# Audio tower on one core: centring and variance of chunks two and three of the output projection placed in the feed-forward loop

## Chip, cores and metric

The kernel runs on one core of one Trainium2 chip. The metric is the time of one execution on the device in microseconds (us), from the first to the last instruction; lower is better. Engines are named as in the profile: PE is TensorE, DVE VectorE, ACT ScalarE, POOL GpSimd, SP SyncE, which issues most DMAs. "Slow" and "full" clock of PE are its two granted levels, 1.2 and 2.4 GHz (0.50 and 1.00 in the profile).

## What is computed

Three blocks run over 2048 tokens (32 sequences of 64) with 1024 features: a token block (projection, layernorm, five-tap convolution, feed-forward), attention, and a grouped feed-forward. The change lies between the last two:

```python
h = tok(x)                                             # 2048 x 1024
h = h + attn(layernorm(h), w_qkv, b_qkv, w_o, b_o)     # ends in vals @ w_o.T + b_o
h = h + ffn(layernorm(h), up, down, perm)

def _layernorm(x, axis=-1, eps=1e-05):
    m = jnp.mean(x, axis=axis, keepdims=True)
    v = jnp.var(x, axis=axis, keepdims=True)
    return (x - m) / jnp.sqrt(v + eps)

def ffn(x, up, down, perm):                            # 16 heads, 64 -> 256 -> 64
    t = x[:, perm].reshape(-1, 16, 64)
    t = einsum('bhd,hdm->bhm', t, up)
    t = gelu(t)
    t = einsum('bhm,hmd->bhd', t, down)
    return t.reshape(-1, 1024)[:, argsort(perm)]
...
```

## The kernel before, in words

Features lie on the 128 partitions in 8 blocks (k or m = 0 to 7), tokens along the free axis in 4 chunks (c = 0 to 3) of 512. All matrix work is fp32; the projections split each operand into a high and a low part and take three matmuls per product (`split3`). Each engine runs its own written-out program, and semaphores alone tie them together, so the order of lines in an engine's block is the order on its queue.

**Projection stage** (780 to 889 us of the profile). For each chunk PE runs three groups of output blocks (0-2, 3-5, 6-7). DVE's `o_evac` (L1350) adds bias and residual into `h2[c % 2]`; SP stores that to HBM (`h2_s[c]`). The sum over features is made by POOL (`o_sum` L737, blocks 1 to 4) and then DVE (`o_sum` L1358, blocks 5 to 7); PE turns it into a mean (`stat_mean_pe` L383) in the next chunk, and ACT copies it out (`stat_copy_act` L370). The deviations of chunk c - 1 are then worked out during chunk c, block by block: DVE centres (`stat_center` L377), ACT squares (L381), POOL adds the squares up (`ln_var_add` L335). The buffer `sq` between them has two slots, so DVE waits for POOL from the third block on. PE reduces the result (`stat_var_pe` L397, eight matmuls of one column into bank 3 here), ACT takes the root (L406), DVE the reciprocal (L410), and SP stores it and reads it back broadcast (`d_stat_load`, tiles `mtd`, `rtd`).

**Feed-forward loop** (889 us to the end): 32 steps s = 8c + a. In step s PE runs `ff_up` of block s + 1 (L1795) into banks 0-3, and `ff_down` of block s (L1804) into bank 4 or 5; ACT runs four gelus (L1077); DVE adds the result of step s - 1 to the gathered block (`d_add` L1408) and prepares a block of the next chunk (`d_prep` L1377, L1384); POOL issues the scatter of the finished block (L758) and the gather (L752), an indirect DMA of 256 KB, of a block of the chunk after. `hg` holds two chunks. Chunk 3's centring runs in this loop, a block per step from s = 5 (`STAT_FROM`), its mean on PE at s = 1 and its variance matmuls at s = 12. Chunk 2's centring runs in the projection of chunk 3, its variance matmuls behind that projection's last group, and the second half of `ff_up` of block 0, which needs bank 3, waits for its root.

Of the kernel before, what the change touches and what calls it, by code (L numbers as in the profile page):

```python
# [32 lines left out]
def audio_tower(nc, x_t, w_proj, w_ff, w_gen, w_qkv_t, w_o_t, up, down, vecs, perm, *outs):  # L33
# [12 lines left out]
    with ctx:  # L46
# [5 lines left out]
        def sem(name):  # L52
# [98 lines left out]
        hg = place("hg", [P, 2 * KB, N], F32, R2 + 16 * KIB)  # L151
# [20 lines left out]
        ln_pool, ln_mean, ln_d, ln_sq, ln_var, ln_std, ln_rstd = (  # L172
            sem(s) for s in ("ln_pool", "ln_mean", "ln_d", "ln_sq", "ln_var", "ln_std", "ln_rstd"))
# [130 lines left out]
        def ln_sum_pool(g, L, blk):  # L304
            g.tensor_tensor(acc[:, :], blk(0), blk(1), ALU.add).then_inc(ln_pool, 1)
            for k in range(2, KB):
                since(g, ln_pool, L, 14, k - 1)
                g.tensor_tensor(acc[:, :], acc[:, :], blk(k), ALU.add).then_inc(ln_pool, 1)  # L308

        def ln_mean_pe(pe, L):  # L310
            since(pe, ln_pool, L, 14, 7)
# [8 lines left out]
        def ln_square_act(act, L, k, d):  # L320
            since(act, ln_d, L, 8, k + 1)
            if k >= 2:
                since(act, ln_pool, L, 14, 7 + max(1, k - 2))
# [5 lines left out]
        def ln_var_add(g, L, k):  # L329

            since(g, ln_sq, L, 8, k + 1)
            if k > 1:
                since(g, ln_pool, L, 14, 7 + k - 1)
            t = squares(L)
            g.tensor_tensor(vacc[:, :], t[:, 0, :] if k == 1 else vacc[:, :], t[:, k % 2, :],  # L335
                            ALU.add).then_inc(ln_pool, 1)
# [5 lines left out]
        def ln_var_pe(pe, L):  # L342
            since(pe, ln_pool, L, 14, 14)
# [28 lines left out]
        def stat_center(e, L, S, k, src):  # L372
            if k == 0:
                since(e, st_copied, S, 1, 1)
            if k >= 2:
                since(e, ln_pool, L, 14, 7 + max(1, k - 2))
            e.tensor_tensor(sq[:, k % 2, :], src, mean_t[:, :], ALU.subtract).then_inc(ln_d, 1)  # L377

        def stat_square_act(act, L, k):
            since(act, ln_d, L, 8, k + 1)  # L380
            act.activation(sq[:, k % 2, :], sq[:, k % 2, :], ACT.Square).then_inc(ln_sq, 1)  # L381

        def stat_mean_pe(pe, L):  # L383
            since(pe, ln_pool, L, 14, 7)
# [4 lines left out]
        def stat_var_pe(pe, L, S, b=LN_BANK):  # L389
            since(pe, ln_pool, L, 14, 14)  # L390
# [25 lines left out]
        def _(sp):  # L416
# [213 lines left out]
            for c in range(CH):  # L630
# [10 lines left out]
                if c > 0:  # L641
# [4 lines left out]
            d_stat_load(1)  # L646
            d_stat_load(2)
# [9 lines left out]
        def _(g):  # L657
# [85 lines left out]
            def gather(n, ks=range(KB)):  # L743
# [1150 lines left out]
```

## Time and profile before

| | |
|---|---|
| median of 3 runs | 1031.88 us (1027.65 to 1033.29) |
| profiled execution | 1035.96 us, of which the span from first to last instruction 1034.2 us |
| PE busy | 967.4 us, 94% of the span |
| DVE, ACT, POOL busy | 509.2, 424.4, 394.3 us |
| DMA | 124.96 MB, 121 GB/s on average |

Times in the rows below are microseconds from the span's start in the profiled execution. A row of a timeline has start, duration, engine, line of the code, operation, output<-inputs, count, and in brackets the idle time of the engine just before and what ended it. Rows of consecutive equal instructions are merged. A fp32 matmul shows as two entries, so `ff_up` of one block (4 matmuls) is x8, and so is `ff_down`.

### The profile page before, as it was taken

What the parts mean: (1) busy time and instruction counts of PE and PEld (TensorE: products, weight loads), DVE (VectorE), ACT (ScalarE), POOL (GpSimd) and SP (SyncE); (2) the same over time, 40 slices, a digit from 0 to 9 for tenths busy, and PEclk for the clock granted to TensorE, in tenths of its full rate; (3) what the DMA queues carried; (4) which work ended last, traced back from release to release, by engine and by line L of the source; (5) the groups of instructions that cost most, each with busy time, mean ns of one, the idle gap of its engine ahead of it and who ended that gap; (6) DMA issues with size and microseconds to landing.
All of it is one profiled execution on the core that took longest, in us unless ns stands there. A gap on an engine that the chain in (4) does not pass through costs nothing.

```text
span 1034.2 us, 15644 instructions
## 1 busy us (share of the span) xinstructions
PE 967.4 (94%) x6108; PEld 714.5 (69%) x6108; DVE 509.2 (49%) x848; ACT 424.4 (41%) x753; POOL 394.3 (38%) x317
## 2 busy tenths in 40 slices
PE   7999999987899999999879999999999999889996
PEld 5777777776777788778657877877887777323331
DVE  6153535659447502254756256256064567755551
ACT  6144444555433533434243243243132332356553
POOL 1225252227601122723361451451023377748532
PEclk9999999999899999999989999999999999899998
DMA  8542725395343154327100201200214975533421
GB/s 290 209 165 4 205 7 181 4 285 203 117 145 107 62 126 164 109 95 265 41 11 22 92 11 35 79 11 22 92 52 149 289 260 209 184 111 133 149 77 61
DMA packets 75062, 124.96 MB, mean 121 GB/s; under 512 B 29159, under 2 KB 38375, under 8 KB 70894
## 3 DMA queue, kind: packets, MB, share of 16 engines
q1 hardware_dynamic: 68830, 107.03, 33.7%
q0 software_dynamic: 5120, 16.78, 4.6%
q8 instruction: 48, 0.79, 0.3%
q10 hardware_dynamic: 1040, 0.16, 0.1%
q14 instruction: 24, 0.20, 0.1%
HBM read 81.46 MB, written 42.50 MB: 120 GB/s over the span
## 4 chain that ended last, share of the span: by engine, by line
PE 53%; issue 10%; POOL 7%; DVE 5%; DMA 3%; ACT 2%; another core or an unknown queue 1%; POOLq 0%; SPq 0%; DVEq 0%; ACTq 0%
PE bank L299 14%; PE bank L301 13%; PE bank L300 13%; PE bank L1795 3%; PE bank L1804 3%; POOL vacc L335 2%; PE bank L1551 1%; POOL out L758 1%; POOL acc L363 1%; DVE sq L377 1%; DMA stage<-w_qkv_t 1%; POOL acc L308 1%; DVE acc L1219 1%; PE bank L1523 1%; DMA db_late<-h_s 1%
## 5 line engine op out<-in xcount | busy, mean ns | idle before, releaser
L335 POOL TENSOR_TENSOR vacc<-vacc,sq 128x512 f32<-128x512 f32 x72 | 97.2, 1350 | 45.8 <-ACT sq L381 36.4
L299 PE MATMUL bank<-xa_h,wp_h 128*128 128x512 f32 x256 | 103.4, 404 | 7.2 <-DVE xa_l L1094 7.2
L299 PE MATMUL bank<-cv_h,wf_h 128*128 128x512 f32 x256 | 106.3, 415 | 1.2 <-POOL wf_l L293 1.2
L301 PE MATMUL bank<-cv_h,wf_l 128*128 128x512 f32 x256 | 101.4, 396 | 0.0
L300 PE MATMUL bank<-cv_l,wf_h 128*128 128x512 f32 x256 | 101.4, 396 | 0.0
L300 PE MATMUL bank<-xa_l,wp_h 128*128 128x512 f32 x256 | 101.1, 395 | 0.0
L301 PE MATMUL bank<-xa_h,wp_l 128*128 128x512 f32 x256 | 101.1, 395 | 0.0
L700 POOL TENSOR_TENSOR fo<-fo,res 128x512 f32<-128x512 f32 x32 | 43.5, 1373 | 123.4 <-ACT fo L837 89.8
L1077 ACT ACTIVATE gt<-bank 128x512 f32<-128x512 f32 x128 | 66.2, 600 | 39.0 <-PE bank L1795 36.8
L1795 PE MATMUL bank<-dd,up_f 64*128 64x512 f32 x256 | 67.9, 651 | 5.6 <-ACT gt L1077 5.4
L381 ACT ACTIVATE sq<-sq 128x512 f32<-128x512 f32 x56 | 35.1, 632 | 79.3 <-DVE sq L377 79.3
L1804 PE MATMUL bank<-gt,dn_f 128*64 128x512 f32 x256 | 62.5, 611 | 0.0
L299 PEld LDWEIGHTS bank<-xa_h,wp_h 128*128 128x128 f32 x256 | 48.9, 191 | 18.9 <-DVE xa_l L1094 7.2
L299 PEld LDWEIGHTS bank<-cv_h,wf_h 128*128 128x128 f32 x256 | 48.9, 191 | 14.1 <-issue 2.8
L299 PE MATMUL bank<-xc_h,wq_h 128*128 128x512 f32 x128 | 54.3, 425 | 3.9 <-issue 3.9
L300 PEld LDWEIGHTS bank<-xa_l,wp_h 128*128 128x128 f32 x256 | 49.0, 191 | 10.8 <-issue 0.7
L301 PEld LDWEIGHTS bank<-cv_h,wf_l 128*128 128x128 f32 x256 | 48.9, 191 | 10.7
L301 PEld LDWEIGHTS bank<-xa_h,wp_l 128*128 128x128 f32 x256 | 48.9, 191 | 10.6
L300 PEld LDWEIGHTS bank<-cv_l,wf_h 128*128 128x128 f32 x256 | 49.0, 191 | 10.5 <-issue 1.2
L758 POOL DMA_INDIRECT out<-hg,rows x32 | 35.3, 1103 | 53.5 <-DVE hg L1408 51.4
L1795 PEld LDWEIGHTS bank<-dd,up_f 64*128 64x128 f32 x256 | 22.4, 194 | 47.9 <-issue 42.2
L1408 DVE TENSOR_TENSOR hg<-bank,hg 128x512 f32<-128x512 f32 x32 | 22.1, 690 | 66.2 <-PE bank L1804 60.1
(179 smaller groups left out, 2167.5 us busy)
## 6 DMA issues: line engine op xcount, KB each, us to landing
xs<-x_t SPq DMA_DIRECT2D x32, 256.0 KB, 6.2
h_s<-ho SPq DMA_DIRECT2D x8, 1024.0 KB, 5.9
res<-h_s SPq DMA_DIRECT2D x32, 256.0 KB, 3.6
h_s<-fo SPq DMA_DIRECT2D x32, 256.0 KB, 2.4
dc<-h_s SPq DMA_DIRECT2D x4, 2048.0 KB, 9.3
h<-h_s SPq DMA_DIRECT2D x8, 1024.0 KB, 10.5
h_s<-h SPq DMA_DIRECT2D x8, 1024.0 KB, 4.8
stage<-w_qkv_t SPq DMA_DIRECT2D x24, 256.0 KB, 3.6
```

The lines of the kernel that those rows point to most:

```text
L299: pe.matmul(o, wh, xh, start=start, stop=False)
L300: pe.matmul(o, wh, xl, start=False, stop=False)
L301: return pe.matmul(o, wl, xh, start=False, stop=stop)
L308: g.tensor_tensor(acc[:, :], acc[:, :], blk(k), ALU.add).then_inc(ln_pool, 1)
L335: g.tensor_tensor(vacc[:, :], t[:, 0, :] if k == 1 else vacc[:, :], t[:, k % 2, :], ALU.add).then_inc(ln_pool, 1)
L381: act.activation(sq[:, k % 2, :], sq[:, k % 2, :], ACT.Square).then_inc(ln_sq, 1)
L700: g.tensor_tensor(fo[m % 4][:, :], fo[m % 4][:, :], res[:, m % 2, :], ALU.add).then_inc(ff_add, 1)
L758: g.indirect_dma_start(out=outs[c], out_offset=bass.IndirectOffsetOnAxis(ap=rows[:, k:k + 1], axis=0), in_=hg[:, hg_block(c) + k, :], in_o ...
L1077: act.activation(gt[a % 2][:, i, :], bank[i][:, :], ACT.Gelu).then_inc(gelu_ok, 1)
L1408: v.tensor_tensor(dst, bank[4 + a % 2][:, :], dst, ALU.add).then_inc(d_ev, 1)
L1795: mm = pe.matmul(bank[2 * blk + j][:, :], up_f[r, a, cols], dd[r, a, :], start=True, stop=True)
L1804: pe.matmul(bank[4 + a % 2][side, :], dn_f[:, FFB * a + 2 * head + blk, :], gt[a % 2][:, i, :], start=blk == 0, stop=blk == 1).then_inc(g_ ...
```

## The change

Chunks are counted from 0, so the third and fourth are c = 2 and 3. Centring of both runs in the loop, two blocks a step, at s = 0 to 3 (c = 2) and s = 8 to 11 (c = 3), into a tile of eight slots, `sq8`. ACT squares them one step later, POOL adds them two steps later. The variance matmuls stand behind steps 6 and 14, in bank 7, the first followed by chunk 3's mean. The semaphore `ln_pool` is split in two (`ln_sum`, `ln_vac`), since sums and variances no longer alternate. `hg` becomes three buffers; the gather of chunk 1 moves from behind the projection into it, ahead of POOL's sum of chunk 3. The preparation of chunk 0 is wholly in the projection of chunk 3, ahead of the evacuations of groups 0 and 1. DVE's `o_sum` moves ahead of the last `o_low`. The store and read-back of chunk 2's deviations move behind `d_stat_load(1)`. Preparation and gather in the loop start a step later (4 and 5 for 3 and 4).

```diff
-        hg = place("hg", [P, 2 * KB, N], F32, R2 + 16 * KIB)
+        hg = [place(f"hg{i}", [P, KB, N], F32, at)
+              for i, at in enumerate((R2 + 32 * KIB, R1 + 48 * KIB, R2 + 16 * KIB))]
+        sq8 = place("sq8", [P, KB, N], F32, E + 16 * KIB)
...
         def ln_var_add(g, L, k):
             since(g, ln_sq, L, 8, k + 1)
             if k > 1:
-                since(g, ln_pool, L, 14, 7 + k - 1)
+                since(g, ln_vac, L, 7, k - 1)
...
         def stat_center(e, L, S, k, src):
             if k == 0:
                 since(e, st_copied, S, 1, 1)
-            if k >= 2:
-                since(e, ln_pool, L, 14, 7 + max(1, k - 2))
-            e.tensor_tensor(sq[:, k % 2, :], src, mean_t[:, :], ALU.subtract).then_inc(ln_d, 1)
+            if L == 3 * CH - 1:
+                since(e, ln_vac, L - 1, 7, max(1, k))
+            elif L < 3 * CH - 2 and k >= 2:
+                since(e, ln_vac, L, 7, max(1, k - 2))
+            dst = sq8[:, k, :] if L >= 3 * CH - 2 else sq[:, k % 2, :]
+            e.tensor_tensor(dst, src, mean_t[:, :], ALU.subtract).then_inc(ln_d, 1)
...
# SP
-                if c > 0:
+                if 0 < c < CH - 1:
                     stat_store(CH + c - 2, 1)
...
             d_stat_load(1)
+            stat_store(2 * CH - 3, 1)
             d_stat_load(2)
...
# POOL
                 if n == 1:
+                    g.wait_ge(qk_mm, 8 * CH)
+                if n == 2:
                     g.wait_ge(o_mm, 8 * CH)
                 for k in ks:
-                    if n >= 2:
-                        g.wait_ge(d_st[k], 16 * (n - 1))
+                    if n == 3:
+                        g.wait_ge(d_st[k], 32)
...
                 if c == 3:
                     gather(0, range(4, KB))
-                ln_var_pool(g, 2 * CH + c - 1)
+                    gather(1)
+                if c < CH - 1:
+                    ln_var_pool(g, 2 * CH + c - 1)
                 o_sum(c)
-            gather(1)
             for s in range(CH * KB + 1):
-                k = s - STAT_FROM
-                if 0 < k < KB:
-                    ln_var_add(g, 3 * CH - 1, k)
+                for i, steps in enumerate(CENTERS):
+                    for k in steps.get(s - 2, ()):
+                        if k > 0:
+                            ln_var_add(g, 3 * CH - 2 + i, k)
...
# ACT
-                    for k in range(KB):
+                    for k in range(KB if c < CH - 1 else 0):
                         stat_square_act(act, L, k)
...
                 gelus(s // KB, s % KB)
-                if s == 2:
+                for i, steps in enumerate(CENTERS):
+                    for k in steps.get(s - 1, ()):
+                        stat_square_act(act, L - 1 + i, k)
+                if s == VAR_AT[0] + 1:
+                    stat_std_act(act, L - 1, FF_VAR_BANK)
                     stat_copy_act(act, L, 2 * CH - 2)
-                if 0 <= s - STAT_FROM < KB:
-                    stat_square_act(act, L, s - STAT_FROM)
-                if s == STAT_FROM + KB:
-                    stat_std_act(act, L)
+                if s == VAR_AT[1] + 1:
+                    stat_std_act(act, L, FF_VAR_BANK)
...
# DVE
-                if c > 0:
+                if 0 < c < CH - 1:
                     o_center(c - 1, range(4))
+                if c == CH - 1:
+                    d_prep(0, range(4))
                 o_evac(c, A_GROUPS[0])
-                for k in range(4, KB) if c > 0 else ():
-                    o_center(c - 1, [k])
-                    if c == CH - 1:
-                        d_prep(0, [k - 4])
+                if 0 < c < CH - 1:
+                    o_center(c - 1, range(4, KB))
+                if c == CH - 1:
+                    d_prep(0, range(4, KB))
                 o_evac(c, A_GROUPS[1])
                 if c + 1 < CH:
                     o_low(c + 1, range(PAIRS - 1))
                 o_evac(c, A_GROUPS[2])
+                o_sum(c)
                 if c + 1 < CH:
                     o_low(c + 1, [PAIRS - 1])
-                o_sum(c)
...
-                d_prep(0, LAST_PREP.get(s, ()))
-                if s == 0:
-                    stat_recip_dve(v, 3 * CH - 2)
-                if 0 <= s - STAT_FROM < KB:
-                    o_center(CH - 1, [s - STAT_FROM])
-                if s == STAT_FROM + KB:
-                    stat_recip_dve(v, 3 * CH - 1)
+                for i, steps in enumerate(CENTERS):
+                    o_center(CH - 2 + i, steps.get(s, ()))
+                    if s == VAR_AT[i] + 2:
+                        stat_recip_dve(v, 3 * CH - 2 + i)
...
# PE
-                        if c > 0 and (g, k) == (2, 3):
+                        if 0 < c < CH - 1 and (g, k) == (2, 3):
                             pe.wait_ge(o_ev, 8 * c + VAR_BANK + 1)
                             stat_var_pe(pe, 2 * CH + c - 1, CH + c - 2, VAR_BANK)
...
             for blk in range(2):
-                if blk == VAR_BANK // 2:
-                    pe.wait_ge(ln_std, 3 * CH - 1)
                 ff_up(0, 0, blk)
...
-                if s == 1:
+                for i in range(2):
+                    if s == VAR_AT[i]:
+                        stat_var_pe(pe, 3 * CH - 2 + i, 2 * CH - 3 + i, FF_VAR_BANK)
+                if s == VAR_AT[0]:
                     stat_mean_pe(pe, 3 * CH - 1)
-                if s == STAT_FROM + KB - 1:
-                    stat_var_pe(pe, 3 * CH - 1, 2 * CH - 2)
...
-LAST_PREP = {0: (4, 5), 1: (6, 7)}
-PREP_AFTER, STAT_FROM, GATHER_AFTER = 3, 5, 4
+CENTERS = ({0: (0, 1), 1: (2, 3), 2: (4, 5), 3: (6, 7)},
+           {8: (0, 1), 9: (2, 3), 10: (4, 5), 11: (6, 7)})
+VAR_AT, FF_VAR_BANK = (6, 14), 7
+PREP_AFTER, GATHER_AFTER = 4, 5
```

## Rows read from the trace of the kernel before

**Rows 1.** The page, section 1: busy time, share of the span, instructions

```profile
PE 967.4 (94%) x6108; PEld 714.5 (69%) x6108; DVE 509.2 (49%) x848; ACT 424.4 (41%) x753; POOL 394.3 (38%) x317
```

**Rows 2.** Timeline of PE where the projection ends and the loop begins

```profile
881.77 0.39 PE L301 MATMUL bank<-vs_h,wo_l 128*128 128x512 f32 x1
886.91 2.00 PE L397 MATMUL bank<-mean_w,vacc 128*128 128x1 f32 x8 [4.75 <-DVE h L1354]
...
894.58 1.94 PE L1804 MATMUL bank<-gt,dn_f 128*64 128x512 f32 x8
```

**Rows 3.** Timelines of POOL and DVE over the same boundary

```profile
882.10 1.71 POOL L335 TENSOR_TENSOR vacc<-vacc,sq 128x512 f32<-128x512 f32 x1 [1.29 <-ACT sq L381]
...
885.60 3.38 DVE L1354 SCALAR_TENSOR_TENSOR h<-bank,vec,h 128x512 f32<-128x512 f32 x5
```

**Rows 4.** Windows of 2 us: busy by engine, PE clock, DMA share, GB/s

```profile
874.00:876.00 2.00, 2.00 (x11) 1.65 (x10) 1.97 (x3) 0.63 (x1) 0.76 (x1) 1.00 0.00 0
...
888.00:890.00 2.00, 2.00 (x8) 1.47 (x10) 0.98 (x2) 1.04 (x2) 1.71 (x3) 0.50 1.03 375
...
902.00:904.00 2.00, 2.00 (x10) 0.55 (x10) 0.69 (x1) 0.00 (x0) 1.40 (x2) 1.00 0.92 327
...
910.00:912.00 2.00, 2.00 (x8) 0.52 (x6) 0.00 (x0) 1.31 (x3) 0.00 (x0) 0.50 0.21 74
```

**Rows 5.** Timeline of PE and ACT in the loop's first steps

```profile
900.23 1.12 PE L385 MATMUL bank<-acc,mean_w 128*128 128x512 f32 x2
...
904.01 0.60 ACT L370 ACTIVATE mean_t<-bank 128x512 f32<-128x512 f32 x1 [4.32 <-remote]
...
908.01 2.93 PE L1795 MATMUL bank<-dd,up_f 64*128 64x512 f32 x8 [2.87 <-ACT gt L1077]
910.87 2.67 PE L1804 MATMUL bank<-gt,dn_f 128*64 128x512 f32 x8
```

**Rows 6.** Timeline of PE late in the loop: two steps, and its end

```profile
1011.54 1.99 PE L1795 MATMUL bank<-dd,up_f 64*128 64x512 f32 x8
...
1015.33 1.99 PE L1795 MATMUL bank<-dd,up_f 64*128 64x512 f32 x8
...
1021.03 3.65 PE L1804 MATMUL bank<-gt,dn_f 128*64 128x512 f32 x16
```

**Rows 7.** Timeline of PE around the variance matmuls of step 12, and the window behind

```profile
946.85 2.01 PE L1795 MATMUL bank<-dd,up_f 64*128 64x512 f32 x8 [0.58 <-ACT gt L1077]
...
951.16 2.03 PE L397 MATMUL bank<-mean_w,vacc 128*128 128x1 f32 x8 [0.44 <-POOL vacc L335]
953.12 3.60 PE L1795 MATMUL bank<-dd,up_f 64*128 64x512 f32 x8
...
954.00:956.00 2.00, 2.00 (x8) 0.63 (x4) 0.00 (x0) 1.74 (x3) 1.70 (x2) 0.50 0.69 212
```

**Rows 8.** Windows of 4 us behind the variance matmuls of chunks 0 and 1

```profile
830.00:834.00 4.00, 4.00 (x18) 3.48 (x19) 4.00 (x4) 0.78 (x2) 3.71 (x3) 1.00 0.21 75
...
858.00:862.00 4.00, 4.00 (x12) 3.11 (x11) 3.56 (x4) 0.59 (x2) 3.71 (x3) 0.60 0.04 13
```

**Rows 9.** Timeline of POOL: a gather in the projection, the eight of chunk 1 (first, last)

```profile
867.47 1.26 POOL L752 DMA_INDIRECT hg<-h_s,rows  x1 [0.30 <-issue]
...
892.41 0.96 POOL L752 DMA_INDIRECT hg<-h_s,rows  x1
...
901.44 0.95 POOL L752 DMA_INDIRECT hg<-h_s,rows  x1 [0.30 <-issue]
```

**Rows 10.** DMA issues: output<-input, queue, count, us from issue to landing

```profile
hg<-h_s,rows POOLq DMA_INDIRECT x32, 5.4
```

**Rows 11.** Timelines of ACT and POOL in the loop: table load, four gelus, one addition

```profile
951.58 1.28 ACT L406 ACT_TABLE_LOAD   x1
...
959.73 2.06 ACT L1077 ACTIVATE gt<-bank 128x512 f32<-128x512 f32 x4 [1.89 <-PE bank L1795]
...
949.82 1.28 POOL L335 TENSOR_TENSOR vacc<-vacc,sq 128x512 f32<-128x512 f32 x1
```

More of the change, by code:

```diff
@@ L171, in audio_tower @@
         a_st = [sem(f"a_st{g}") for g in range(2)]
-        ln_pool, ln_mean, ln_d, ln_sq, ln_var, ln_std, ln_rstd = (
-            sem(s) for s in ("ln_pool", "ln_mean", "ln_d", "ln_sq", "ln_var", "ln_std", "ln_rstd"))
+        ln_sum, ln_vac, ln_mean, ln_d, ln_sq, ln_var, ln_std, ln_rstd = (
+            sem(s) for s in ("ln_sum", "ln_vac", "ln_mean", "ln_d", "ln_sq", "ln_var", "ln_std", "ln_rstd"))
         st_copied, mean_st, rstd_st = sem("st_copied"), sem("mean_st"), sem("rstd_st")
@@ L304, in ln_sum_pool @@
         def ln_sum_pool(g, L, blk):
-            g.tensor_tensor(acc[:, :], blk(0), blk(1), ALU.add).then_inc(ln_pool, 1)
+            g.tensor_tensor(acc[:, :], blk(0), blk(1), ALU.add).then_inc(ln_sum, 1)
             for k in range(2, KB):
-                since(g, ln_pool, L, 14, k - 1)
-                g.tensor_tensor(acc[:, :], acc[:, :], blk(k), ALU.add).then_inc(ln_pool, 1)
+                since(g, ln_sum, L, 7, k - 1)
+                g.tensor_tensor(acc[:, :], acc[:, :], blk(k), ALU.add).then_inc(ln_sum, 1)
         def ln_mean_pe(pe, L):
-            since(pe, ln_pool, L, 14, 7)
+            since(pe, ln_sum, L, 7, 7)
             since(pe, ln_std, L - 1, 1, 1)
@@ L322, in ln_square_act @@
             if k >= 2:
-                since(act, ln_pool, L, 14, 7 + max(1, k - 2))
+                since(act, ln_vac, L, 7, max(1, k - 2))
             act.activation(squares(L)[:, k % 2, :], d, ACT.Square).then_inc(ln_sq, 1)
@@ L332, in ln_var_add @@
             if k > 1:
-                since(g, ln_pool, L, 14, 7 + k - 1)
-            t = squares(L)
-            g.tensor_tensor(vacc[:, :], t[:, 0, :] if k == 1 else vacc[:, :], t[:, k % 2, :],
-                            ALU.add).then_inc(ln_pool, 1)
+                since(g, ln_vac, L, 7, k - 1)
+            t, at = (sq8, k) if L >= 3 * CH - 2 else (squares(L), k % 2)
+            g.tensor_tensor(vacc[:, :], t[:, 0, :] if k == 1 else vacc[:, :], t[:, at, :],
+                            ALU.add).then_inc(ln_vac, 1)
         def ln_var_pool(g, L):
@@ L342, in ln_var_pe @@
         def ln_var_pe(pe, L):
-            since(pe, ln_pool, L, 14, 14)
+            since(pe, ln_vac, L, 7, 7)
             since(pe, ln_d, L, 8, 8)
@@ L361, in stat_sum_pool @@
             if k > 1:
-                since(g, ln_pool, L, 14, k - 1)
-            g.tensor_tensor(acc[:, :], blk(0) if k == 1 else acc[:, :], blk(k), ALU.add).then_inc(ln_pool, 1)
+                since(g, ln_sum, L, 7, k - 1)
+            g.tensor_tensor(acc[:, :], blk(0) if k == 1 else acc[:, :], blk(k), ALU.add).then_inc(ln_sum, 1)
         def stat_copy_act(act, L, S):
@@ L374, in stat_center @@
                 since(e, st_copied, S, 1, 1)
-            if k >= 2:
-                since(e, ln_pool, L, 14, 7 + max(1, k - 2))
-            e.tensor_tensor(sq[:, k % 2, :], src, mean_t[:, :], ALU.subtract).then_inc(ln_d, 1)
+            if L == 3 * CH - 1:
[4 more added lines that the diff above has]
+            e.tensor_tensor(dst, src, mean_t[:, :], ALU.subtract).then_inc(ln_d, 1)
         def stat_square_act(act, L, k):
             since(act, ln_d, L, 8, k + 1)
-            act.activation(sq[:, k % 2, :], sq[:, k % 2, :], ACT.Square).then_inc(ln_sq, 1)
+            d = sq8[:, k, :] if L >= 3 * CH - 2 else sq[:, k % 2, :]
+            act.activation(d, d, ACT.Square).then_inc(ln_sq, 1)
         def stat_mean_pe(pe, L):
-            since(pe, ln_pool, L, 14, 7)
+            since(pe, ln_sum, L, 7, 7)
             pe.matmul(bank[LN_BANK][:, :], mean_w[:, :], acc[:, :], start=True, stop=True).then_inc(ln_mean, 1)
         def stat_var_pe(pe, L, S, b=LN_BANK):
-            since(pe, ln_pool, L, 14, 14)
+            since(pe, ln_vac, L, 7, 7)
             since(pe, st_copied, S, 1, 1)
@@ L922, in b_step @@
                     act.wait_ge(mean_st, 16 * (CH - 1))
-                    act.wait_ge(ln_pool, 14 * (CH - 1))
+                    act.wait_ge(ln_vac, 7 * (CH - 1))
                 if c == 1:
@@ L1361, in o_sum @@
                     v.wait_ge(o_ev, 8 * c + m + 1)
[L1362 to L1363 removed]
+                    v.wait_ge(ln_sum, 7 * (2 * CH + c) + m - 1)
+                    v.tensor_tensor(acc[:, :], acc[:, :], h2[c % 2][:, m, :], ALU.add).then_inc(ln_sum, 1)
             def o_center(c, ks):
```

18 lines of the change are left out of this document (7 added, 11 removed).

## Prediction

> **What bounds the kernel now.** I read the page's busy times first: PE is busy 94% of the span [rows 1], so time can come back only where PE stands still, works at the slow clock, or does side work. Then PE's timeline from the last projection on, for every gap above 0.3 us, and the windows of 2 us for its clock and the DMAs. A step of the loop takes 3.79 us at full clock (1011.54 to 1015.33), and the last `ff_down` ends at 1021.03 + 3.65 = 1024.68 [rows 6]. From the first `ff_down`, at 894.58 [rows 2], 32 steps of which the last has no `ff_up` would take 31 x 3.79 = 117.3 us; they take 130.1. Four places hold what is lost:
>
> - **The boundary.** The projection's last matmul ends at 882.16. PE then stands 4.75 us, runs chunk 2's variance matmuls for 2.0 us, and reaches the first `ff_down` at 894.58, 12.4 us later [rows 2]. What ends the wait is DVE's evacuation, five blocks at once at 885.60 that could have been done as banks filled [rows 3]; it had stood behind the centring, and that behind POOL's additions, 1.71 us each and 1.29 us of wait between [rows 3]. The clock is at 0.50 when the loop starts [rows 4].
> - **First steps.** The mean costs 1.06 us. Then ACT gets it only at 904.01, 2.7 us after PE's record ends, released by something the trace doesn't name; PE stands 2.87 us, and the next step takes 2.93 + 2.67 for 3.79 [rows 5], at clock 0.50 [rows 4]. I call this the **unnamed stall**: 2.87 + 1.7 = 4.6 us.
> - **Centring of chunk 3.** With two slots, DVE, ACT and POOL go in lockstep, and every second step PE waits 0.58 us for a gelu [rows 7]; four or five such waits make 2.5 us.
> - **Variance at step 12**: 0.44 us of wait, 2.0 us of matmuls, and an `ff_up` of 3.60 us for 1.99 behind them, at clock 0.50: 4.1 us [rows 7].
>
> 1.1 + 4.6 + 2.5 + 4.1 = 12.3 of the 12.8 us lost in the loop.
>
> **The change, part by part.**
>
> *Boundary.* DVE has no centring left there, only preparations and evacuations at 0.68 us each [rows 3]. `ff_up` of block 0 needs bank 3 evacuated by 882.16 and a prepared block, and `ff_down` banks 4 to 7 by 884.1. With preparation ahead of evacuation, DVE needs eight operations for blocks 4 to 7 (5.4 us) and one evacuation (0.7) after those gathers have landed: free if they land by 876.0. The fourth is issued at 867.47 [rows 9] and lands 5.4 us later by the median of all gathers [rows 10]; in the kernel before the DMA engines had nothing left in flight at 874 [rows 4]. Cost 0, at most 1 us, since chunk 1's gathers queue behind. Then `ff_up` of block 0 starts at 882.16 and takes 1.9 us; by the pattern of the loop its gelus start 1.2 us in and the first two end at 884.4, `ff_up` of block 1 runs to 886.4, and the first `ff_down` starts there, not at 894.58. PE never idles over 0.5 us, so I take the clock as full. **Gain 8.2 us** (7 to 8.5).
>
> *What POOL does instead.* It loses seven additions and issues twelve gathers in a row ahead of its sum of chunk 3. The first four end at 868.7; eight more at 1.29 us (892.41 to 901.44, seven intervals) or at the 1.56 us of the row in the projection end at 879.0 to 881.2 [rows 9]. Four additions of 1.28 [rows 11] to 1.71 us [rows 3] end at 884.1 to 888.0; DVE's three behind them, 2.0 us, at 886.2 to 890.1. **Queued behind that wait on DVE** are the first centrings, behind these on ACT two squares, and behind those the gelus of block 2, which `ff_up` of block 3 wants at about 892.1. Counting back two gelus, two squares and two centrings (1.0, 1.2, 1.3) the sum must be over by 888.4. Cost 0 to 1.7 us, and I take 0, because the gathers in one unbroken row are the nearer case to the eight at 1.29.
> The 2 MB of these gathers fall into a time when the DMA engines are idle (0.00 at 874 to 876) and leave one when they carry 327 GB/s (902 to 904) [rows 4].
>
> *The unnamed stall.* It stands in the middle of the eight gathers' traffic and the read-backs of the statistics. Both are gone from there. I take it as gone, with 3 in 10 that it is of another making and comes again.
>
> *Mean* moved: 1.06 us either way. *Variance*: one group leaves the boundary (counted), one is new behind step 6, one moves from 12 to 14. Each is 2.0 us of matmuls, and a clock that falls: 1.6 us at `ff_up` [rows 7], and the same for a group in the projection, 0.60 in the window behind chunk 1's, but not behind chunk 0's, 1.00 [rows 8]. Two groups: 4.0 + 3.2 = 7.2 us for 3.6 before. The wait for POOL: after step 6 it has finished long before. For step 14, POOL has in steps 10 to 13 seven additions and four pairs of scatter and gather. At 1.28 and 2 x 1.3 us that is 19 us, at 1.71 and 2 x 1.56 us 24 us; the last pair stands behind the last addition, so 16.8 to 21.3 us count against 4 steps and a step's own length, 18.9 us: 0 to 2.4 us of wait. I take 0.
> POOL's addition takes 1.71 us beside DVE in the projection [rows 3] and 1.28 us in the loop [rows 11]. The Trainium skill, page "GPSIMD Engine Reference", section "Key points", says that POOL shares its SBUF interfaces with VectorE and contends with DVE instructions that have two SBUF inputs. That speaks against this change, which puts two such centrings a step beside the additions; by it the upper figures would hold, and the sum be about 2 us longer.
>
> *Lockstep.* With eight slots DVE waits for no addition. DVE's step holds at most five operations, 3.4 us, and ACT's four gelus and two squares, 2.06 [rows 11] + 1.2 = 3.3 us, both under 3.79, and each engine's urgent work comes first in its step. Gain 2.5 us and the 0.44. The two more table loads, 1.28 us each [rows 11], fall where ACT has over 1.7 us spare and PE is at its variance matmuls: 0, at most 0.5 us.
>
> *Rest.* `o_sum` ahead of the last `o_low`: the mean matmul that PE runs next hides it, 0 (0.3 us at most). SP: `d_stat_load(2)` now waits for a reciprocal at step 8, is needed at step 12, 15 us for a store and a load. `d_stat_load(1)` no longer waits. Gathers for the third buffer come seven steps before use. All 0.
>
> **The sum.** First `ff_down` 886.4; + 117.3 + 1.1 (mean) + 7.2 (variance) + 0.5 (unassigned before) = 1012.5 for the end of PE, against 1024.68: **12.2 us**. The tail behind it (9.5 us, scatters landing) stays. The profiled execution would go from 1035.96 to 1023.8. That execution lies 4.1 us above the median, about one unnamed stall, so the median runs may never have had it: then their gain is 7.6 us. 1031.88 - 12.2 = 1019.7, 1031.88 - 7.6 = 1024.3. I forecast **1021.5 us**, nearer to the first.
>
> **The rivals.**
>
> 1. *The stall comes again* (or is absent from the median of before, same result): 1024.3. For it: the trace doesn't name its releaser. Against: its place in the DMA traffic.
> 2. *The clock holds behind the variance groups.* 3.2 us less, 1016.5 to 1018. For it, chunk 0's group [rows 8]; against it, the other two. By the Trainium skill, page "TensorE: Matmul & The Clock Gate", section "Why this matters for your kernels", throughput drops come from long idle gaps between bursts of matmuls; by that the clock would hold here, where PE idles 0.44 us at most.
> 3. *POOL becomes the bound.* Upper prices in both places: 1.7 + 2.4 us, and a fallen clock behind each wait, 3.3 us: 1027 to 1029, within 0.5% of before. For it: POOL's rows of 1.71; against: POOL's additions in the loop all near 1.28.
> 4. *Slower: the evacuation stands behind late gathers.* DVE's preparation of blocks 4 to 7 is in front of the evacuation of banks 3 to 7, and PE waits us for us once they land after 876.0. The gain is used up at 888, and over 0.5% lost if they land after 893, 25 us after issue: 1038 or more. Against: 5.4 us by the median [rows 10].
> 5. *The change doesn't do what it says*: PE still stands at the boundary for some other evacuation, at half of the gain: 1026. DVE's free time of 2.7 us there speaks against it.
>
> **How the numbers follow.** Forecast case 0.5, rival 1 0.2, rival 2 0.12, rival 3 with rival 5 0.13, rival 4 0.05. Each case carries some 2 us of scatter, as the runs before lie between 1027.65 and 1033.29. Range 1015.5 to 1027.5: it takes in rivals 1 and 2 whole and part of 3. A measurement of this kernel can tell about 0.5% from no change, 5.2 us: faster means below 1026.7. Faster 0.88 (all of the forecast, 1 and 2, and a part of 3 and 5), same 0.08, slower 0.04.
>
> **What the profile would show.** Right: PE's first `ff_up` within 1 us of the last projection matmul, clock 1.00 there; POOL with twelve gathers in a row, over by 881; no wait of DVE's L377 on POOL in the loop, steps of 3.79 us in centring; two L397 groups in the loop, each with a step near 5.4 us behind it; no `remote` wait. Wrong: an idle PE before L1795 ended by DVE's L1377 or L1354 (rival 4 or 5), by ACT in steps 2 and 3 (POOL's sum late), or before the second L397 by POOL (rival 3).

## The result

The changed kernel takes 1021.53 us in the median of 6 runs (1018.15 to 1023.42), the kernel before 1031.95 us in the median of 6 (1027.65 to 1033.29): ratio 0.9905, 95% interval 0.9885 to 0.9925, 10.4 us faster. The forecast was 1021.5 us. The profiled execution took 1021.69 us, its span 1020.0 us, against 1034.2 before.

The page after, section 1 (busy time, share, instructions), answers to [rows 1]: PE's busy time is what it was, its share is one point higher.

```profile
PE 967.3 (95%) x6108; PEld 717.8 (70%) x6108; DVE 510.6 (50%) x848; ACT 426.5 (42%) x755; POOL 394.3 (39%) x317
```

PE's timeline after, at the boundary, answers to [rows 2]. The last projection matmul ends at 882.40, the loop's first `ff_up` follows at once, and the first `ff_down` is there 4.3 us after the projection, where it was 12.4 us.

```profile
882.01 0.39 PE L303 MATMUL bank<-vs_h,wo_l 128*128 128x512 f32 x1
882.33 1.99 PE L1807 MATMUL bank<-dd,up_f 64*128 64x512 f32 x8
884.73 2.02 PE L1807 MATMUL bank<-dd,up_f 64*128 64x512 f32 x8 [0.42 <-ACT gt L1088]
886.68 1.94 PE L1816 MATMUL bank<-gt,dn_f 128*64 128x512 f32 x8
```

The windows there (columns as in [rows 4]) have the clock at 1.00, and the DMA engines are busy at 876, where they had been idle (share 0.01 from 876 to 878 in the profile before):

```profile
876.00:878.00 2.00, 2.00 (x11) 1.65 (x10) 2.00 (x5) 0.00 (x0) 1.69 (x2) 1.00 0.83 287
...
888.00:890.00 2.00, 2.00 (x12) 0.69 (x8) 1.31 (x3) 1.27 (x3) 0.34 (x1) 1.00 0.58 182
```

POOL and DVE ahead of the boundary, timelines after, answer to [rows 3] and [rows 9]: twelve gathers from 862.50 to 878.29, the four additions over at 883.88, DVE's part of the sum at 886.28. DVE waited 0.25 us for the last gathered block that it prepares.

```profile
862.50 0.96 POOL L761 DMA_INDIRECT hg<-h_s,rows  x1
...
877.34 0.95 POOL L761 DMA_INDIRECT hg<-h_s,rows  x1 [0.31 <-issue]
...
879.75 4.13 POOL L365 TENSOR_TENSOR acc<-acc,h 128x512 f32<-128x512 f32 x3
...
874.92 0.69 DVE L1390 TENSOR_TENSOR dd<-hg,mtd 128x512 f32<-128x512 f32 x1 [0.25 <-DMA hg<-h_s,rows]
...
883.99 2.29 DVE L1376 TENSOR_TENSOR acc<-acc,h 128x512 f32<-128x512 f32 x3 [0.74 <-POOL acc L365]
```

In the loop PE has no wait of its own from step 1 on. Its timeline at the two variance groups and at the end answers to [rows 6] and [rows 7]; the last row is of POOL, whose last two additions end at 943.77, 0.7 us ahead of the second group.

```profile
911.26 2.03 PE L403 MATMUL bank<-mean_w,vacc 128*128 128x1 f32 x8
913.15 1.10 PE L391 MATMUL bank<-acc,mean_w 128*128 128x512 f32 x2
914.18 1.99 PE L1807 MATMUL bank<-dd,up_f 64*128 64x512 f32 x8
...
944.46 2.03 PE L403 MATMUL bank<-mean_w,vacc 128*128 128x1 f32 x8
946.42 2.82 PE L1807 MATMUL bank<-dd,up_f 64*128 64x512 f32 x8
949.16 2.76 PE L1816 MATMUL bank<-gt,dn_f 128*64 128x512 f32 x8
...
1006.76 3.65 PE L1816 MATMUL bank<-gt,dn_f 128*64 128x512 f32 x16
...
940.80 2.97 POOL L337 TENSOR_TENSOR vacc<-vacc,sq 128x512 f32<-128x512 f32 x2
```

A measure that serves below is the time from the end of the last projection matmul to the end of the last `ff_down`, one profile each. It leaves out the stages ahead, which do the same work in every kernel here and yet end anywhere between 879.9 and 887.3 us, kernels with the same program there included. "Fall" is what the slow clock behind a variance group in the loop took. The ratio is to the kernel before on the same chip.

| kernel | end of projection to end of PE, us | of it fall | ratio to before (95%) |
|---|---|---|---|
| before | 142.5 | 1.6 | |
| b_again | 138.2 | 1.5 | 1.0002 (0.9979 to 1.0025) |
| b_spread | 136.3 | 0 | 1.0003 (0.9981 to 1.0025) |
| b_mean | 136.3 | 0 | 1.0007 (0.9981 to 1.0032) |
| b8_proj | 136.5 | 1.6 | 0.9991 (0.9971 to 1.0012) |
| b8_front | 139.9 | 1.6 | 1.0037 (1.0016 to 1.0058) |
| b_tiny | 131.9 | 1.6 | 0.9952 (0.9924 to 0.9979) |
| b_evac | 138.7 | 0 | 1.0037 (1.0014 to 1.0061) |
| b8_loop | 138.6 | 0 | 0.9993 (0.9969 to 1.0017) |
| b_sqlate | 134.2 | 1.6 | 0.9969 (0.9950 to 0.9989) |
| after | 128.0 | 1.6 | 0.9905 (0.9885 to 0.9925) |
| a_sqnow | 131.0 | 0 | 0.9962 (0.9941 to 0.9984) |
| a_burst | 128.0 | 1.6 | 0.9933 (0.9908 to 0.9957) |
| a_row | 124.7 | 0 | 0.9889 (0.9865 to 0.9914) |

### The profile page after: what moved, and what is told of

Read it like the earlier page. It is cut to its first block, busy times and chain, and to the rows that moved or that the text cites. A ratio compares the mean times of both kernels' runs of the same rounds, so it can differ in the third digit from the quotient of the medians.

```text
span 1020.0 us, 15647 instructions
## 1 busy us (share of the span) xinstructions
PE 967.3 (95%) x6108; PEld 717.8 (70%) x6108; DVE 510.6 (50%) x848; ACT 426.5 (42%) x755; POOL 394.3 (39%) x317
## 4 chain that ended last, share of the span: by engine, by line
PE 63%; issue 8%; POOL 4%; DMA 2%; DVE 2%; ACT 1%; POOLq 0%; SPq 0%; ACTq 0%; DVEq 0%
PE bank L301 15%; PE bank L302 14%; PE bank L303 14%; PE bank L1807 6%; PE bank L1816 6%; POOL vacc L337 2%; PE bank L1563 1%; PE bank L1535 1%; DVE acc L1232 1%; POOL acc L310 1%; DMA stage<-w_qkv_t 1%; PE bank L1689 1%; PE bank L1716 1%; DMA db_late<-h_s 1%; PE bank L403 1%
## 5 line engine op out<-in xcount | busy, mean ns | idle before, releaser
L1807 PE MATMUL bank<-dd,up_f 64*128 64x512 f32 x256 | 64.5, 622 | 0.4 <-ACT gt L1088 0.4
L303 PEld LDWEIGHTS bank<-xa_h,wp_l 128*128 128x128 f32 x256 | 48.6, 190 | 10.4
L301 PE MATMUL bank<-wv_h,xc_h 128*128 128x512 f32 x128 | 51.2, 400 | 2.2 <-DVE wv_l L295 2.2
L301 PE MATMUL bank<-vs_h,wo_h 128*128 128x512 f32 x128 | 52.8, 413 | 0.4 <-ACT vo L998 0.4
```

The lines of the kernel that those rows point to most:

```text
L301: pe.matmul(o, wh, xh, start=start, stop=False)
L303: return pe.matmul(o, wl, xh, start=False, stop=stop)
L1807: mm = pe.matmul(bank[2 * blk + j][:, :], up_f[r, a, cols], dd[r, a, :], start=True, stop=True)
```

## The experiments

### Was the unnamed stall in the median?

**b_again**: the kernel before, unchanged.

> The kernel before, profiled once more. If the unnamed stall (PE idle 2.87 us ahead of the loop's third step, ACT's copy of the mean 2.7 us late) is a fixed part of this program, the second profile has it at the same place, a span near 1034. If it is an accident of the first profile, it is absent, the span is near 1030, and the 12.2 us of the forecast have 4.6 us that the median never paid. Ratio 1.00 either way.

Its span is 1028.5 us, and in its loop no wait of PE, ACT or DVE has an unnamed releaser. PE's timeline (the same places as [rows 2], [rows 7], [rows 6]):

```profile
885.54 2.00 PE L397 MATMUL bank<-mean_w,vacc 128*128 128x1 f32 x8 [4.75 <-DVE h L1354]
887.47 6.22 PE L1795 MATMUL bank<-dd,up_f 64*128 64x512 f32 x16
893.62 1.94 PE L1804 MATMUL bank<-gt,dn_f 128*64 128x512 f32 x8
...
945.59 2.03 PE L397 MATMUL bank<-mean_w,vacc 128*128 128x1 f32 x8 [0.44 <-POOL vacc L335]
947.55 3.48 PE L1795 MATMUL bank<-dd,up_f 64*128 64x512 f32 x8
...
1015.31 3.65 PE L1804 MATMUL bank<-gt,dn_f 128*64 128x512 f32 x16
```

From the projection to the first `ff_down` 12.8 us, and 138.2 in all: 4.3 less than in the first profile, which is the stall. It is no fixed part of the program. From here on this profile is the one to compare with.

**b_spread**: chunk 1's gathers halved.

```diff
-            gather(1)
+            gather(1, range(4))
             for s in range(CH * KB + 1):
...
                     scatter((s - 1) // KB, (s - 1) % KB)
+                if 0 < s < 5:
+                    gather(1, [3 + s])
```

> The kernel before with the eight gathers of chunk 1 halved: four ahead of the loop, four one by one in steps 1 to 4. Theory (the burst of gathers and read-backs makes the unnamed stall): the stall goes, 3 to 4.6 us faster. Rival (it is of another making, such as the mean on PE or the start of the loop): the stall stays, within 1 us of before.

No stall, 136.3 us, which is b_again without the fall, to 0.4 us. Since b_again has no stall either, the profile tells nothing of the cause; the ratio, 1.0003, says that the burst costs the median at most 0.2%.

**b_mean**: chunk 3's mean two steps later on PE and ACT.

```diff
# PE
-                if s == 1:
+                if s == 3:
                     stat_mean_pe(pe, 3 * CH - 1)
# ACT
-                if s == 2:
+                if s == 4:
                     stat_copy_act(act, L, 2 * CH - 2)
```

> The kernel before with chunk 3's mean on PE at step 3 for step 1 and ACT's copy of it at step 4 for step 2. Theory (burst of gathers): the stall stays near 900 to 908 us, ended by something else than the copy, time as before. Rival (the mean behind a half-warm loop makes it): the stall moves two steps, 7.6 us later, with the mean. If it vanishes, 3 to 4.6 us faster.

No stall, 136.3 us again, no change of the time. Waits that the trace puts down to nothing it knows came back in four other profiles, of kernels that issue the eight gathers at the loop's start (b8_loop, b8_front, b_evac, b_tiny), always in steps 2 to 4, on DVE and mostly on ACT as well; only in b8_loop did they cost PE over 1 us. DVE's timeline and PE's in that run:

```profile
907.46 0.69 DVE L1411 TENSOR_TENSOR hg<-bank,hg 128x512 f32<-128x512 f32 x1 [5.21 <-remote]
...
907.76 2.02 PE L1798 MATMUL bank<-dd,up_f 64*128 64x512 f32 x8 [2.14 <-ACT gt L1080]
```

They are in none of the four profiles of the changed kernel and its variants, a_burst among them. With the first profile that makes five of the nine profiles in which the kernel before or a variant of it issues the whole burst in the loop, and none of the other five, though a_burst issues the burst in the loop too. What holds the engines there stays open.

### What held the boundary?

**b8_proj**: eight slots for chunk 2's deviations, all else as before.

```diff
         def stat_center(e, L, S, k, src):
             if k == 0:
                 since(e, st_copied, S, 1, 1)
-            if k >= 2:
+            if k >= 2 and L != 3 * CH - 2:
                 since(e, ln_pool, L, 14, 7 + max(1, k - 2))
-            e.tensor_tensor(sq[:, k % 2, :], src, mean_t[:, :], ALU.subtract).then_inc(ln_d, 1)
+            dst = sq8[:, k, :] if L == 3 * CH - 2 else sq[:, k % 2, :]
+            e.tensor_tensor(dst, src, mean_t[:, :], ALU.subtract).then_inc(ln_d, 1)
...
```

> The kernel before with eight slots for chunk 2's deviations, still centred in the projection of chunk 3. Theory (the boundary's idle time is the lockstep of DVE, ACT and POOL over two slots): seven additions of 1.3 to 1.7 us end at 881, before the projection does, PE's 4.75 us of idle time go and the clock stays full: 6 us faster, with the 2.0 us of variance matmuls left at the boundary. Rival (the DVE's evacuations end the wait, and stand behind other work all the same): under 2 us.

Ratio 0.9991 (0.9971 to 1.0012): no change clear of noise, where 6 us were expected. DVE, POOL and PE, timelines of b8_proj:

```profile
880.52 1.78 DVE L379 TENSOR_TENSOR sq<-h,mean_t 128x512 f32<-128x512 f32 x1
...
880.02 1.74 POOL L336 TENSOR_TENSOR vacc<-vacc,sq 128x512 f32<-128x512 f32 x1 [1.89 <-ACT sq L384]
...
887.88 2.00 PE L400 MATMUL bank<-mean_w,vacc 128*128 128x1 f32 x8 [3.33 <-DVE h L1357]
```

DVE waits for no slot now, and the centring still takes 1.78 us, where it takes 0.68 alone. It begins 0.5 us into POOL's addition and ends 0.5 us behind it. With the two operations of a preparation that is 3.03 us a block, the pace of the kernel before. The slots were not what set this pace. They bought something smaller: PE idles 3.33 us here and 4.75 us in every profile of the kernels that keep two slots and the other work of the boundary (before, b_again, b_spread, b_mean, b8_loop, b_sqlate), 1.4 us less. That is 0.14% of the time, which the ratio neither shows nor excludes.

**b_tiny**: POOL's additions of chunk 2's squares on 8 columns. The sum over the other 504 is left out, so this kernel doesn't compute the layernorm of chunk 2.

```diff
         def ln_var_add(g, L, k):
...
             t = squares(L)
+            if isinstance(L, int) and L == 3 * CH - 2:
+                g.tensor_tensor(vacc[:, 0:8], t[:, 0, 0:8] if k == 1 else vacc[:, 0:8], t[:, k % 2, 0:8],
+                                ALU.add).then_inc(ln_pool, 1)
+                return
```

> The kernel before with POOL's seven additions of chunk 2's squares, in the projection of chunk 3, on 8 columns for 512 (the rest of that sum is left out); two slots and all waits stay. Theory A (DVE's centring is stretched from 0.68 to 1.78 us because it overlaps POOL's addition): each centring takes 0.68 us, DVE's evacuations end with the projection, PE's 4.75 us of idle time and the slow start go, 6 to 7 us faster. Theory B (DVE is late through its waits for the two slots alone): the waits shrink as well, so the gain is alike, but the centrings behind which no wait lay in the run with eight slots stay at 1.78 us.

Theory A held. DVE, POOL and PE of b_tiny:

```profile
880.86 0.69 DVE L381 TENSOR_TENSOR sq<-h,mean_t 128x512 f32<-128x512 f32 x1
...
871.63 0.21 POOL L336 TENSOR_TENSOR vacc<-sq 128x8 f32<-128x8 f32 x1 [1.78 <-ACT sq L385]
...
880.25 0.69 DVE L1388 TENSOR_TENSOR dd<-dd,rtd 128x512 f32<-128x512 f32 x1
880.36 0.64 POOL L336 TENSOR_TENSOR vacc<-vacc,sq 128x8 f32<-128x8 f32 x1 [1.29 <-ACT sq L385]
...
884.37 1.80 PE L401 MATMUL bank<-mean_w,vacc 128*128 128x1 f32 x8
```

Every centring takes 0.68 to 0.69 us, PE idles none ahead of its variance matmuls, and the time from the projection on is 131.9 us, 6.3 less than in b_again; ratio 0.9952, some 5 us. The two slots stay.

The edit shortens two things at once, POOL's additions and what they cost DVE, and the rows tell them apart. From the first centring to the end of the last addition b_again takes 19.6 us (865.86 to 885.44), b_tiny 13.4 (869.59 to 882.95). Of the 6.2 us, 4.1 are the last four centrings, 0.68 or 0.69 us each for 1.53, 1.78, 1.78 and 1.75; 1.1 is the last addition, 0.65 for 1.71; and 1.1 is the one wait of DVE for a slot, 0.99 for 2.07. So the boundary was held by DVE and POOL hindering each other: two thirds of what this edit freed were DVE's operations stretched beside POOL's additions, the rest the additions themselves and the wait for them.

The stretch goes both ways: POOL's addition takes 1.28 to 1.71 us and DVE's operation 0.68 to 1.78. An addition on 8 columns takes 0.21 us where DVE stands idle (871.63), and 0.64 where it begins 0.1 us into a preparation of DVE's, ending 0.06 us behind it. Whichever begins second loses about what is left of the other: POOL 0.43 us there with 0.58 left, DVE 1.1 us in b8_proj with 1.2 left. The Trainium skill, page "GPSIMD Engine Reference", section "Key points", names a contention of POOL with DVE instructions of two SBUF inputs; the trace agrees, with the figures just given.

**b8_front**: b8_proj with all eight centrings first.

```diff
                 if c > 0:
-                    o_center(c - 1, range(4))
+                    o_center(c - 1, range(4 if c < CH - 1 else KB))
                 o_evac(c, A_GROUPS[0])
                 for k in range(4, KB) if c > 0 else ():
-                    o_center(c - 1, [k])
                     if c == CH - 1:
                         d_prep(0, [k - 4])
+                    else:
+                        o_center(c - 1, [k])
```

> The kernel before with eight slots for chunk 2's deviations, and all eight centrings ahead of the evacuations in the projection of chunk 3, where POOL is still issuing gathers; chunk 0's preparation stands alone between the groups. Theory A: centrings take 0.61 each, the additions run unbroken and end near 881, but DVE's preparations, which now overlap them, stretch to near 1.7 us: DVE's bank 3 is out by 882 to 885, PE idles 0 to 3 us, 3 to 6 us faster. Theory B: preparations stay at 0.68, PE idles none, 6 us faster.

Slower, 1.0037 (3.8 us): both theories expected a gain. In the profile 1.7 us of it lie between the end of the projection and the end of PE (139.9 for 138.2). DVE, POOL and PE of b8_front:

```profile
869.51 9.31 DVE L379 TENSOR_TENSOR sq<-h,mean_t 128x512 f32<-128x512 f32 x8 [2.11 <-ACT mean_t L371]
...
873.31 9.80 POOL L336 TENSOR_TENSOR vacc<-vacc,sq 128x512 f32<-128x512 f32 x6
...
890.39 2.03 PE L400 MATMUL bank<-mean_w,vacc 128*128 128x1 f32 x8 [5.95 <-DVE h L1357]
```

The eight centrings overlap the additions and take 9.31 us for 5; PE idles 5.95 us, more than before. The price of theory A was right, but I had charged it to the preparations alone and not to the centrings, on the ground that POOL was still issuing gathers; it is so only for the first two or three.

**b_evac**: evacuations of banks 3 to 5 in DVE's free time.

```diff
                     if c == CH - 1:
+                        if k > 4:
+                            o_evac(c, [k - 2])
                         d_prep(0, [k - 4])
-                o_evac(c, A_GROUPS[1])
+                if c < CH - 1:
+                    o_evac(c, A_GROUPS[1])
```

> The kernel before with the evacuations of banks 3, 4 and 5 of chunk 3 each put behind the centrings of blocks 5, 6 and 7, in DVE's free time. If the evacuation ends PE's idle time of 4.75 us, as the profile names it, that time falls to 3 us or less. If POOL's last addition ends it (1.71 us from 885.10 in the profile of before, over 0.1 us ahead of PE's start), it stays at 4.7 us; no change of the time.

DVE, POOL and PE of b_evac:

```profile
890.49 0.74 DVE L1354 SCALAR_TENSOR_TENSOR h<-bank,vec,h 128x512 f32<-128x512 f32 x1
...
891.31 1.64 POOL L335 TENSOR_TENSOR vacc<-vacc,sq 128x512 f32<-128x512 f32 x1 [1.89 <-ACT sq L381]
...
893.04 2.00 PE L397 MATMUL bank<-mean_w,vacc 128*128 128x1 f32 x8 [5.74 <-issue]
```

Bank 5 is out at 891.23, bank 3 some 7 us earlier, and PE starts 0.09 us behind the end of POOL's last addition, 892.95. In the kernel before that addition is

```profile
885.10 1.71 POOL L335 TENSOR_TENSOR vacc<-vacc,sq 128x512 f32<-128x512 f32 x1 [1.29 <-ACT sq L381]
```

It ends at 886.81, 0.10 us ahead of PE's start at 886.91. It had been POOL's addition, not the evacuation that the profile names, that ended PE's wait. The idle time grew to 5.74 us: the rounds that took 3.03 us take 4.67, 3.53 and 3.53 us (centrings at 881.69, 886.36 and 889.89), by the evacuation's 0.74 us and because POOL's addition now meets the second operation of the preparation, 1.67 us for 0.69. The kernel became 0.4% slower.

### What held the loop's centring steps?

**b8_loop**: the edit of b8_proj with `L == 3 * CH - 1`, chunk 3 in the loop, for `L == 3 * CH - 2`.

> The kernel before with eight slots for chunk 3's deviations in the loop. Forecast's step (the two slots make PE's 0.58 us waits): they go, 2.5 us faster. Rival (POOL's step of an addition, a scatter and a gather, 3.9 to 4.2 us, is longer than PE's 3.79, and the variance at step 12 waits for its last addition whatever the slots): the short waits go, the wait ahead of the variance matmuls grows from 0.44 to about 3 us, no change.

No change, 0.9993, but the rival's mechanism is not there either. PE keeps the same four waits, 0.69, 0.68, 0.59 and 0.58 us, the first of which is

```profile
919.91 2.01 PE L1798 MATMUL bank<-dd,up_f 64*128 64x512 f32 x8 [0.69 <-ACT gt L1080]
```

and the wait ahead of the variance matmuls stays at 0.45 us. Neither the slots nor POOL set this pace. PE waits for a gelu; ACT's timeline of the kernel before says why it is late:

```profile
923.84 0.63 ACT L381 ACTIVATE sq<-sq 128x512 f32<-128x512 f32 x1 [1.21 <-DVE sq L377]
924.37 2.04 ACT L1077 ACTIVATE gt<-bank 128x512 f32<-128x512 f32 x4
```

ACT stands idle for a square whose centring is the last thing DVE does in the same step, and the next gelus are queued behind it. This wait is no slot's: ACT had been told to square in the step of the centring.

**b_sqlate**: the kernel before, squares and all that follows them one step later.

```diff
# ACT
-                if 0 <= s - STAT_FROM < KB:
-                    stat_square_act(act, L, s - STAT_FROM)
-                if s == STAT_FROM + KB:
+                if 0 <= s - STAT_FROM - 1 < KB:
+                    stat_square_act(act, L, s - STAT_FROM - 1)
+                if s == STAT_FROM + KB + 1:
                     stat_std_act(act, L)
# POOL
-                k = s - STAT_FROM
+                k = s - STAT_FROM - 1
...
```

> The kernel before, still with two slots and one block a step, but ACT squares chunk 3's deviations one step after DVE centres them, not in the same step; additions, variance matmuls (step 13 for 12), root and reciprocal follow a step later. Theory (ACT waits in each step for DVE's centring of that very step, and the next gelus stand behind the square): PE's four waits of 0.58 to 0.69 us go, 2.5 us faster, 0.2%. Rival (POOL sets the pace at 3.9 to 4.2 us a step through the two slots): the waits stay or move, no change.

0.9969, 3.2 us faster, with the two slots kept. All waits of PE in the loop are gone, and ACT waits for PE instead of DVE:

```profile
924.66 0.63 ACT L381 ACTIVATE sq<-sq 128x512 f32<-128x512 f32 x1
926.39 2.06 ACT L1077 ACTIVATE gt<-bank 128x512 f32<-128x512 f32 x4 [1.11 <-PE bank L1795]
```

**a_sqnow**: the converse in the changed kernel.

```diff
-                    for k in steps.get(s - 1, ()):
+                    for k in steps.get(s, ()):
                         stat_square_act(act, L - 1 + i, k)
```

> The changed kernel with ACT's squares in the same step as the centrings, for both chunks; all else as changed. Theory of the square's place: in each of the eight centring steps the gelus of the next step stand behind two squares that wait for DVE, in the second set behind a preparation too; PE waits 0.5 to 2 us a step, 6 us slower than the changed kernel, ratio to before 0.996. Rival (the eight slots brought the gain in the loop): no waits on PE, ratio 0.990 as the changed kernel.

0.9962, with the eight slots in place. Waits of 0.27 us in the first set and 1.35, 1.29 and 1.11 in the second, as in

```profile
922.10 1.23 ACT L387 ACTIVATE sq<-sq 128x512 f32<-128x512 f32 x2 [2.48 <-DVE sq L382]
...
924.45 2.01 PE L1807 MATMUL bank<-dd,up_f 64*128 64x512 f32 x8 [1.35 <-ACT gt L1088]
```

From the projection on it takes 131.0 us without a fall, 4.6 more than the changed kernel without its fall; by the two ratios it is 5.9 us slower. So the place of the square is worth some 3 us with one block a step and 5 to 6 with two, and it is the part of the change that cleared the loop. Whether two blocks a step could have done with two slots no run shows.

### The moved gathers, and a cheaper variance

**a_burst**: chunk 1's gathers back at the loop's start.

```diff
                     gather(0, range(4, KB))
-                    gather(1)
...
                 o_sum(c)
+            gather(1)
             for s in range(CH * KB + 1):
```

> The changed kernel with the eight gathers of chunk 1 put back behind POOL's sum of chunk 3, at the loop's start; three buffers stay. Theory (after the second profile of before: their place cost nothing): POOL is free again near 891, catches up on the additions with the first scatter late by 2 us, the first variance matmuls wait 0 to 3 us; within 3 us of the changed kernel. Rival (the burst in the loop makes the unnamed stall, once in a few executions): a wait on PE of over 2 us in steps 1 to 4 and 4 us slower than the changed kernel.

POOL issues them at 885.17 to 895.25 and has added the squares up at 911.11, 2.8 us ahead of the first variance group. From the projection on PE takes 128.0 us, as in the changed kernel. The ratio is 0.9933, and its interval overlaps the changed kernel's; a difference of some 3 us isn't excluded, but this profile has none of it where the two kernels differ. Its projection ends 2.6 us later than the changed kernel's, and it was 2.6 us late already at chunk 1's variance group (858.60 for 855.97), ahead of the first gather.

```profile
885.17 0.95 POOL L761 DMA_INDIRECT hg<-h_s,rows  x1
...
908.15 2.96 POOL L337 TENSOR_TENSOR vacc<-vacc,sq 128x512 f32<-128x512 f32 x2
...
913.86 2.03 PE L403 MATMUL bank<-mean_w,vacc 128*128 128x1 f32 x8
```

**a_row**: both variance reductions of the loop as one matmul of 512 columns; ACT's root and DVE's reciprocal then go over 512 columns too, and chunk 3's centring and variance stand one step later.

```diff
         def stat_var_pe(pe, L, S, b=LN_BANK):
             since(pe, ln_vac, L, 7, 7)
             since(pe, st_copied, S, 1, 1)
+            if L >= 3 * CH - 2:
+                pe.matmul(bank[b][:, :], mean_w[:, :], vacc[:, :], start=True, stop=True).then_inc(ln_var, 1)
+                return
...
-           {8: (0, 1), 9: (2, 3), 10: (4, 5), 11: (6, 7)})
-VAR_AT, FF_VAR_BANK = (6, 14), 7
+           {9: (0, 1), 10: (2, 3), 11: (4, 5), 12: (6, 7)})
+VAR_AT, FF_VAR_BANK = (6, 15), 7
```

> The changed kernel with each of the two variance reductions in the loop as one matmul of 512 columns for four of one column: the result is a row, ACT takes its root and DVE its reciprocal over 512 columns (3.35 us for 0.17, by the rows of the attention stage), and chunk 3's centring starts at step 9 for 8, its variance at 15 for 14, so that DVE has room. Theory (side work on PE costs what it lasts, and the clock falls behind groups of one column only): 2 x 1.0 us less on PE and no fall of the clock, 2 to 3.6 us faster than the changed kernel, ratio to before 0.987 to 0.9885. Rival (DVE's long reciprocal holds up the addition of a block or the centring, and PE waits for it): no gain or slower, with PE waiting in steps 9 or 17.

1019.14 us in the median, ratio 0.9889, the fastest of all, though its interval overlaps the changed kernel's. In the profile:

```profile
915.15 1.13 PE L399 MATMUL bank<-vacc,mean_w 128*128 128x512 f32 x2
916.11 1.02 PE L391 MATMUL bank<-acc,mean_w 128*128 128x512 f32 x2
917.06 1.99 PE L1816 MATMUL bank<-dd,up_f 64*128 64x512 f32 x8
...
922.92 3.34 DVE L423 RECIPROCAL rstd<-rstd 128x512 f32<-128x512 f32 x1
```

A reduction takes 1.0 us of PE for 1.9, the clock falls behind neither, and PE waits nowhere for the reciprocal, 3.34 us on DVE: 124.7 us from the projection on for 128.0.

## Why the prediction was right, and where not

The point was hit in part by luck. Against b_again the profile has 138.2 - 128.0 = 10.2 us of gain, and the medians 10.4. The prediction's sum without the stall, which b_again and the ratio of b_spread speak against in the median, gives 7.6 us; 1021.5 came of standing between that and 12.2. The 2.6 us that 7.6 falls short are mostly a fall of the clock that didn't come (1.5 us), the unassigned 0.5 and 0.3 at the boundary. And the cause named for two of the terms was wrong.

- **Boundary: 8.2 us forecast, 8.5 measured** (12.8 to 4.3 from the projection to the first `ff_down`). Right in size and in what PE would do, to 0.3 us. Wrong in the cause: I read POOL's 1.71 us and 1.29 us of wait in [rows 3] as a lockstep over two slots, and the evacuation as what ended PE's wait. b8_proj, b_tiny and b_evac put POOL's addition and its contention with DVE in their place; the slots held 1.4 us of the 4.75. The sum didn't notice, since the change removes the additions and the centrings from the boundary altogether, whichever held it. Who had taken my reading and bought slots would have gained 1.4 us of the 6 expected.
- **The unnamed stall: 4.6 us taken as gone, with rival 1 for its being absent from the median.** Rival 1 held in that second form, though not its time, 1024.3. b_again showed it, as far as one profile and the ratio of b_spread can; it is the one term of the sum that was no fixed property of the kernel, and hedging over it, not knowledge, brought the point to 1021.5.
- **Lockstep: 2.5 + 0.44 us forecast, and PE's waits did go.** The cause named, the two slots, was wrong (b8_loop: nothing). The gain came from a part that I had not priced at all, the square a step behind its centring (b_sqlate 3.2 us, a_sqnow 4.6 us by its profile and 5.9 by the ratios).
- **Variance: 7.2 us forecast, 5.7 paid** (2.03 + 2.03 and one fall of 1.65, from 2.82 + 2.76 for 3.93). Rival 2 half held: the clock stayed up behind the first group.
- **The unassigned 0.5 us** did not recur. (The sum's 31 x 3.79 is 117.5, not 117.3; counted as 30 x 3.79 + 3.65 for the two last `ff_down` it is 117.35.)
- **POOL's burst: 0 forecast, of 0 to 1.7.** The sum ended at 886.3, at the low end of the 886.2 to 890.1 forecast and 2.1 us ahead of the limit of 888.4. The wait at step 14 was 0 as well, but with 0.7 us to spare. Rival 3's prices for POOL were seen in part: additions of 1.49 us in the second set, none at 1.71, and preparations of DVE of up to 2.29 us for 0.68 (at 934.68), for which PE didn't wait.
- **Late gathers (rival 4)**: the last landed at about 874.9, 1.1 us ahead of the limit of 876.0. **Rival 5**: PE ran on at once.

Added up, without the stall: 8.5 at the boundary, 2.5 + 0.44 for the waits, 0.5 unassigned, less 2.0 for the second variance group and 0.15 for a slightly dearer fall is 9.8 of the 10.2 us.

## What to carry to other kernels

Give each instruction that depends on another engine's last work of a step a place one step later, before buying buffers: a square in its centring's own step cost 3 us here with one block a step and 5 to 6 with two, and eight slots for two gave, alone, nothing in the loop and 1.4 us at the boundary. When two engines' operations both stretch while they overlap (0.68 to 1.78 us, 1.28 to 1.71 us), what helped here was to move one of them away; loosening the waits between them gave little (b8_proj), and moving the overlap onto another operation lost time (b8_front, b_evac). And profile a kernel twice before pricing a stall whose releaser the trace can't name.

## What the runs showed of the hardware

**DVE and POOL.** A DVE operation with two SBUF inputs of 128x512 that begins 0.5 us into a POOL addition of that size ends about 0.5 us behind it, 1.78 us for 0.68 (880.52 in b8_proj); the evacuation, which reads one of its inputs from PSUM, keeps its 0.69 to 0.74 us beside the same additions (2.06 us for three at 872.03 in b8_proj).

**The clock behind one-column matmuls.** The clock fell behind 8 of the 16 groups of one-column variance matmuls that ran in the loop in these profiles, and took 1.5 to 1.65 us each time; PE had stood idle 0.45 us at most directly ahead of them. The three groups with the mean matmul of 512 columns right behind them kept the clock; so did both one-matmul groups of a_row, which aren't among the 16. Eight of the thirteen others fell. The Trainium skill, page "TensorE: Matmul & The Clock Gate", section "Why this matters for your kernels", names idle gaps between bursts of matmuls as what to avoid against throughput drops; by that the clock would have held behind all 16, and the traces don't agree. Whether the mean matmul is what kept the clock, three cases don't settle.

**A switch of ACT's tables** cost 1.28 us and nothing behind it: in the changed kernel the load of 914.99 ends at 916.27 and the gelus start at 916.28.

```profile
914.99 1.28 ACT L1088 ACT_TABLE_LOAD   x1
916.28 2.07 ACT L1088 ACTIVATE gt<-bank 128x512 f32<-128x512 f32 x4
```
